# Attention values as four column tiles in one batch per window row, softmax sums inverted once and spread by matmuls

## The chip, the cores and the metric

One NeuronCore of a Trainium2 chip runs the whole program. The time is the device time of one execution in microseconds (us), given as the median of several runs. Engines: TensorE (PE for its matmuls, PEld for its weight loads), VectorE (DVE), ScalarE (ACT), GpSimd (POOL), and SyncE (SP), which only issues DMAs here.

## What is computed

For 32 images of 56x56 pixels with 128 channels, in fp32, two residual blocks one after the other:

```python
x = x + window_attention(group_norm(x))   # 7x7 windows, shifted by 3, 8 heads of 16 channels
x = x + conv3x3(group_norm(x))            # 128 -> 128 channels, weights from signs and clipping
```

Group norm has 32 groups of 4 channels. The attention of one window has N = 49 tokens: `softmax(q k^T / 4 + relative bias + mask) v` for each head, and a 128x128 projection with bias. An image has 8 rows of 8 windows.

## The kernel before, in words

All five engines run one program of images `i` and, in each, 32 units `u`. A unit is one pair of heads (4 pairs) in one row of 8 windows (8 rows). Work of three images is interleaved in a unit: attention of image i, the conv of image i-1, loading and the first norm of image i+1. Every engine has its own `body(i)` with the order of its work written out by hand, and semaphores tie them. TensorE's order in unit u (its `body`, L994 on): scores of two units (only in even u), part of the conv, transposes of the probabilities of unit u-2 (`turn_probs`, L886), the odd jobs placed in the middle of the unit, more conv, then the values of unit u-3 (`values`, L895) before the q, k, v matmuls (`qkv`, L909) in even u and behind them in odd u, more conv, and the odd jobs placed at the end of the unit. Odd jobs (`misc`, L937) share one PSUM bank, `misc_ps`, in a fixed order that `misc_jobs` (L96) lists: turning the attention output ("ot", at u = 7, 11, ...), the projection ("proj", at u = 9, 13, ...), turning loaded and finished tiles ("tin", "tout"), and the group norm's averages ("gn1", "gn2").

The probabilities of a pair of heads lie with 49 queries of an even window at partitions 0 to 48 and of an odd window at 64 to 112. After the transposes `probsT` has, for each window, both heads' 49 keys on the partitions (K of 128 rows, 64 for each head) and 49 queries in the free dimension. `values` takes `probsT` of a window as the weights (128 rows x 49 columns) and V as the moving operand (34 columns: 16 channels of each head, and a column of ones for each head, which gives the softmax sums). Even windows write PSUM partitions 0 to 48, odd ones 64 to 112: two column tiles. After every two pairs VectorE takes reciprocals of the sums (L706) and multiplies (L714, two products), into `o_sb`, tokens on partitions. "ot" transposes `o_sb` of the row by four transposes (L953), ScalarE copies the result to fp16 (`oT_hi`, L472), VectorE makes the remainder (`oT_lo`, L727), and "proj" multiplies with the fp16 weights (high and low parts, three matmuls).

The scores are fp32 with 32 rows x 49 columns of weights and 98 moving columns (L880): two row groups times two column groups of the array. q, k, v and the conv are fp16 in three products (L867, L986). In the trace an fp32 matmul is two pairs of a weight load and a matmul; a transpose and an fp16 matmul are one.

Stores: `x_out` has a slot for each of the 7 tiles of an image; ScalarE copies a finished tile into it (L485) and SP stores it (L352).

Of the kernel before, what the change touches and what calls it, by code (L numbers as in the profile page):

```python
# [26 lines left out]

# [23 lines left out]
VW = 2 * HD + 2  # L51
# [7 lines left out]
SUB = 4  # L59
# [9 lines left out]
LAG_T, LAG_PV = 2, 3  # L69
# [72 lines left out]

def roll_pieces(rows, row0=0):
# [8 lines left out]
def build_block(nc, x, wqkv, bqkv, wproj, bproj, table, wconv, prune, ident_d, group_d, parity_d, mask_d, out):  # L152
    with ExitStack() as ctx:
# [22 lines left out]
        w_in = sb("w_in", [128, 4, C])  # L176
# [3 lines left out]
        w_f = sb("w_f", [128, 4, C])  # L180
# [24 lines left out]
        x_out = sb("x_out", [SP_, TILES * SUB, C])  # L205
# [4 lines left out]
        v = sb("v", [128, 2, NWIN, PAIRS, VW])  # L210
# [46 lines left out]
        x_stored = [sem(f"x_stored{t}") for t in range(TILES)]  # L257
# [13 lines left out]
        attn_norm = sem("attn_norm")  # L271
        oT_hi_ready = sem("oT_hi_ready")
# [21 lines left out]
        wc_u = flat(x_of[1])[:, 0:PLANES * KW * C].rearrange("p (t c) -> p t c", c=C)  # L294
        wc_sum = flat(x_n)[:, 0:C]
# [21 lines left out]
        def _(sp):  # L317
# [24 lines left out]
            def body(i):  # L342
                for u in range(UNITS):
                    for kind, t in misc_at(i, u):
# [4 lines left out]
                        if kind == "tout":  # L349
                            img = i - 1 - tile_turned(t)[0]  # L350
                            sp.wait_ge(misc_free, misc_number(i, kind, t) + 1)
                            sp.dma_start(out_tiles[img, t], x_out[:, t * SUB:(t + 1) * SUB, :]).then_inc(x_stored[t], 16)  # L352

            over_images(sp, body)
            for t in range(TILES):
                sp.wait_ge(x_stored[t], 16 * IMGS)
# [3 lines left out]
        def _(pool):  # L360
# [8 lines left out]
            last.then_inc(rel_ready, 1)  # L369

# [78 lines left out]
        def _(act):  # L449
# [10 lines left out]
            def evacuate_probsT(i, g, slot):  # L460
                act.wait_ge(probsT_ready, g + 1)
                need(act, attn_ready, g - 1)
                nc.scalar.copy(probsT[:, slot % 2], probsT_ps[:].rearrange("p (w n) -> p w n", n=ODD)[:, :, 0:N])\  # L463
                    .then_inc(probsT_sb, 1)

            def misc(i, u, place):
                for kind, t in misc_at(i, u, (place,)):
                    number = misc_number(i, kind, t)
                    if kind == "ot":

                        act.wait_ge(misc_ready, number + 1)
                        nc.scalar.copy(oT_hi[:].rearrange("p r (w c) -> p w r c", c=WIN),  # L472
                                       misc_ps[:].rearrange("p (w n) -> p w n", n=ODD)[:, :, 0:N]
                                       .rearrange("p w (r c) -> p w r c", c=WIN)).then_inc(oT_hi_ready, 1)
# [6 lines left out]
                    if kind == "tout":  # L481
                        img = i - 1 - tile_turned(t)[0]
                        act.wait_ge(misc_ready, number + 1)
                        need(act, x_stored[t], 16 * img)
                        nc.scalar.copy(x_out[:, t * SUB:(t + 1) * SUB, :],  # L485
# [3 lines left out]
            def body(i):  # L489
                for u in range(UNITS):  # L490
# [62 lines left out]
        def _(dve):  # L553
# [12 lines left out]
            for buf, value in ((v, 0.0), (probs, 0.0), (scores_ps, 0.0), (attn_ps, 1.0)):  # L566
# [4 lines left out]
            for e in range(2):  # L571

                step(vec.memset(v[ODD * e:ODD * e + N, :, :, :, 2 * HD + e:2 * HD + e + 1], 1.0))
# [33 lines left out]
            step(vec.tensor_copy(wT_hi[:], w_f[:]))  # L607
            step(vec.tensor_tensor(wT_lo[:], w_f[:], wT_hi[:], ALU.subtract))
# [89 lines left out]
            def body(i):  # L698
                for u in range(UNITS):

                    n, rest = divmod(u - (LAG_PV + 2), 2)
                    if rest == 0 and live(i, 0 if n >= 0 else -1):
                        number, half = i * ROWS * 2 + n, n % 2
                        dve.wait_ge(attn_ready, (number + 1) * 2)
                        outputs = attn_ps[0:QP, 0:WP * 2 * VW].rearrange("p (a v) -> p a v", v=VW)
                        vec.reciprocal(recip[0:QP, half], outputs[:, :, 2 * HD:VW]).then_inc(recip_ready, 1)  # L706
                        dve.wait_ge(recip_ready, number + 1)
                        if half == 0 and (not isinstance(number, int) or number > 0):

                            turn = i if u >= 2 else i - 1  # L710
                            dve.wait_ge(misc_ready, misc_number(turn, "ot", (n // 2 - 1) % ROWS) + 1)
                        for pair in range(2):
                            at = (half * 2 + pair) * 2 * HD
                            last = vec.tensor_tensor(  # L714
                                o_sb[0:QP, :, at:at + 2 * HD].rearrange("p w (e d) -> p w e d", d=HD),
                                outputs.rearrange("p (w a) v -> p w a v", a=2)[:, :, pair, 0:2 * HD]
                                .rearrange("p w (e d) -> p w e d", d=HD),
                                recip[0:QP, half].rearrange("p (w a) e -> p w a e", a=2)[:, :, pair].unsqueeze(3)
                                .to_broadcast((QP, WP, 2, HD)), ALU.mult)
                        last.then_inc(attn_norm, 1)  # L720
                    turn, at = divmod(u - 1, UNITS)
                    for kind, t in misc_at(i + turn, at):
                        if kind == "ot":

                            row = (i + turn) * ROWS + (t if at >= OT_AT else t - ROWS)
                            dve.wait_ge(oT_hi_ready, row + 1)
                            vec.tensor_tensor(oT_lo[:].rearrange("p r (w c) -> p w r c", c=WIN),  # L727
                                              misc_ps[:].rearrange("p (w n) -> p w n", n=ODD)[:, :, 0:N]
                                              .rearrange("p w (r c) -> p w r c", c=WIN),
                                              oT_hi[:].rearrange("p r (w c) -> p w r c", c=WIN), ALU.subtract)\  # L730
                                .then_inc(misc_free, 1)
# [114 lines left out]
        def _(pe):  # L846
# [48 lines left out]
            def values(i, u):  # L895
                g, (r, pair) = i * UNITS + u, divmod(u, PAIRS)
                pe.wait_ge(probsT_sb, g + 1)
                if pair == 0:
                    pe.wait_ge(qkv_free, (i * ROWS + r) * 4 + 4)
                if pair % 2 == 0:  # L900
                    need(pe, attn_norm, (i * ROWS + r) * 2 + pair // 2)
                for w in range(NWIN):
                    p0, wp = ODD * (w % 2), w // 2
                    at = (wp * 2 + pair % 2) * VW
                    last = mm(attn_ps[p0:p0 + N, at:at + VW], probsT[:, u % 2, w, :], v[:, r % 2, w, pair, :],  # L905
                              start=True, stop=True)
# [30 lines left out]
            def misc(i, u, kind, t):  # L937
# [12 lines left out]
                if kind == "ot":  # L950
                    pe.wait_ge(attn_norm, (i * ROWS + (t + 1 if u >= OT_AT else t + 1 - ROWS)) * 2)
# [118 lines left out]
```

## Time and profile before

| | us |
|---|---|
| median of 3 runs | 3638.6 (3636.86 to 3641.4) |
| the profiled execution | 3642.03 |
| its span | 3640.2 |
| matmuls on TensorE | 57227 |
| busy: TensorE, its weight loads | 3423.5 (94%), 2802.9 (77%) |
| busy: VectorE, ScalarE, GpSimd | 3016.5 (83%), 2559.9 (70%), 2293.8 (63%) |

A busy share is the time in which an engine had an instruction under way. Matmul durations are modelled and overlap; their starts are measured. The idle time before a group, with the engine and line that ended it, tells who waited for whom.

### The profile page before, as it was taken

How to read it: one execution, taken by the hardware profiler on the slowest of the kernel's cores; microseconds unless marked ns; L12 is line 12 of the kernel's file. 1: busy time of each engine (PE TensorE's matmuls, PEld its weight loads, DVE VectorE, ACT ScalarE, POOL GpSimd, SP SyncE). 2: the span in 40 equal slices, each digit the busy share in tenths (PEclk: the TensorE clock that was granted, in tenths of full speed). 3: DMA queues.
4: the chain of work that ended last, by engine and by line, in shares of the span. 5: the costliest groups of instructions: out<-in, count | busy, mean ns of one | idle time of the engine just before them, and what ended most of it. 6: DMA issues, size and time to landing. Idle time of an engine off the chain costs nothing.

```text
span 3640.2 us, 140757 instructions
## 1 busy us (share of the span) xinstructions
PE 3423.5 (94%) x57227; PEld 2802.9 (77%) x57227; DVE 3016.5 (83%) x7426; ACT 2559.9 (70%) x5729; POOL 2293.8 (63%) x3674
## 2 busy tenths in 40 slices
PE   2999999999999999999999999999999999999997
PEld 1778778777778777778777778777778778778775
DVE  5788888888888888888888888888888888888875
ACT  1777777777777777777777777777777777777763
POOL 4476666766666766656766666766656766657753
PEclk9999999999999999999999999999999999999999
DMA  2011101111101111101111001111001111101001
GB/s 57 20 30 33 33 25 30 35 33 35 33 25 30 35 33 35 33 23 33 33 35 35 28 28 33 33 35 35 28 28 33 33 35 33 30 25 33 18 18 29
DMA packets 213328, 113.72 MB, mean 31 GB/s; under 512 B 8784, under 2 KB 212688, under 8 KB 212688
## 3 DMA queue, kind: packets, MB, share of 16 engines
q1 hardware_dynamic: 212688, 104.72, 10.1%
q8 instruction: 459, 7.52, 0.8%
q14 instruction: 181, 1.48, 0.1%
HBM read 53.31 MB, written 51.38 MB: 29 GB/s over the span
## 4 chain that ended last, share of the span: by engine, by line
PE 52%; DVE 23%; POOL 12%; issue 10%; ACT 2%; SPq 0%; DVEq 0%; DMA 0%; POOLq 0%; ACTq 0%
PE conv_ps L986 14%; PE qkv_ps L867 11%; PE attn_ps L905 7%; PE probsT_ps L891 7%; PE scores_ps L880 5%; DVE s_sb L738 4%; DVE plane_lo L750 3%; POOL s_sb L402 3%; PE misc_ps L867 2%; DVE x L781 2%; DVE s_max L743 2%; PE misc_ps L953 2%; PE misc_ps L949 2%; PE misc_ps L943 2%; POOL x_n L441 1%
## 5 line engine op out<-in xcount | busy, mean ns | idle before, releaser
L402 POOL TENSOR_TENSOR s_sb<-s_sb,s_max 113x392 f32<-113x392 f32 x1024 | 1000.8, 977 | 1171.4 <-DVE s_max L743 1167.1
L457 ACT ACTIVATE probs<-s_sb 113x392 f32<-113x392 f32 x1024 | 552.4, 539 | 158.4 <-POOL s_sb L402 151.2
L891 PE MATMUL probsT_ps<-ident,probs 113*128 113x113 f32 x4096 | 587.4, 265 | 75.0 <-ACT probsT L463 74.9
L429 POOL TENSOR_TENSOR plane<-x_n 128x224 f32<-128x224 f32 x896 | 600.8, 691 | 18.7
L526 ACT COPY v<-qkv_ps 64x256 f32<-64x256 f32 (+2 forms) x1280 | 393.8, 327 | 300.9 <-PE qkv_ps L867 294.6
L743 DVE TENSOR_REDUCE s_max<-s_sb 113x8 f32<-113x392 f32 x1024 | 574.7, 561 | 35.3
L905 PEld LDWEIGHTS attn_ps<-v,probsT 128*49 128x49 f32 x16384 | 466.0, 125 | 179.0 <-issue 137.4
L463 ACT COPY probsT<-probsT_ps 128x392 f32<-128x392 f32 x1024 | 489.7, 478 | 161.1 <-PE probsT_ps L891 155.8
L738 DVE TENSOR_TENSOR s_sb<-scores_ps,bias 113x392 f32<-113x392 f32 x1024 | 567.6, 554 | 7.6 <-PE scores_ps L880 7.6
L905 PE MATMUL attn_ps<-v,probsT 128*49 128x34 f32 x16384 | 567.2, 214 | 0.4 <-DVE o_sb L714 0.2
L891 PEld LDWEIGHTS probsT_ps<-ident,probs 113*128 113x128 f32 x4096 | 432.6, 142 | 133.7 <-ACT probs L457 87.8
L986 PE MATMUL conv_ps<-plane_hi,wc_hi 128*128 128x224 f16 x2688 | 483.3, 262 | 15.8 <-DVE conv_y L812 11.4
L986 PE MATMUL conv_ps<-plane_hi,wc_lo 128*128 128x224 f16 x2688 | 481.5, 262 | 0.0
L880 PE MATMUL scores_ps<-k,q 32*49 32x98 f32 x16384 | 458.5, 248 | 0.0
L880 PEld LDWEIGHTS scores_ps<-k,q 32*49 32x49 f32 x16384 | 353.3, 119 | 119.8 <-issue 83.4
L986 PE MATMUL conv_ps<-plane_lo,wc_hi 128*128 128x224 f16 x2688 | 409.3, 261 | 18.0 <-DVE plane_lo L750 18.0
L781 DVE SCALAR_TENSOR_TENSOR x<-misc_ps,w_max,x 128x371 f32<-128x371 f32 (+2 forms) x576 | 199.8, 393 | 252.5 <-PE misc_ps L867 252.5
L867 PE MATMUL qkv_ps<-wT_hi,tok_hi 128*128 128x128 f16 (+1 forms) x2304 | 398.2, 227 | 4.4 <-ACT v L526 2.8
L867 PE MATMUL qkv_ps<-wT_lo,tok_hi 128*128 128x128 f16 (+1 forms) x2304 | 389.3, 220 | 0.0
L867 PE MATMUL qkv_ps<-wT_hi,tok_lo 128*128 128x128 f16 (+1 forms) x2304 | 389.3, 220 | 0.0
L441 POOL TENSOR_SCALAR x_n<-x,gn_y,gn_shift 128x371 f32<-128x371 f32 (+2 forms) x576 | 338.4, 597 | 7.6 <-POOL gn_shift L391 7.6
L517 ACT ACTIVATE k<-qkv_ps,k_bias,k_scale 128x392 f32<-128x392 f32 x512 | 321.3, 682 | 13.6 <-PE qkv_ps L867 13.5
(144 smaller groups left out, 6564.2 us busy)
## 6 DMA issues: line engine op xcount, KB each, us to landing
x_in<-in_x_dram SPq DMA_DIRECT2D x224, 224.0 KB, 2.7
out_dram<-x_out SPq DMA_DIRECT2D x224, 224.0 KB, 2.3
x<-in_L_conv_w_dram SPq DMA_DIRECT2D x1, 576.0 KB
x<-L_conv_pruning_mask_dram SPq DMA_DIRECT2D x1, 576.0 KB
x_n<-_conv_rel_pos_table_dram SPq DMA_DIRECT2D x14, 10.7 KB
x_n<-in_mask_dram SPq DMA_DIRECT2D x1, 196.0 KB
w_in<-n_L_conv_qkv_weight_dram SPq DMA_DIRECT2D x1, 192.0 KB
ident<-in_ident_dram SPq DMA_DIRECT2D x1, 64.0 KB
```

What stands on the lines that cost most here:

```text
L402: nc.gpsimd.tensor_tensor(s, s, top, ALU.subtract).then_inc(sub_ready, 1)
L429: last = nc.gpsimd.tensor_tensor(plane[:, t % 2, j], *sums[j])
L457: nc.scalar.activation(probs[0:QP, slot % 2, :, :, 0:N], s_sb[0:QP, slot % 4], ACT.Exp)\
L463: nc.scalar.copy(probsT[:, slot % 2], probsT_ps[:].rearrange("p (w n) -> p w n", n=ODD)[:, :, 0:N])\
L526: last = nc.scalar.copy(v[half, slot, w0:w0 + n, :, e * HD:(e + 1) * HD], vals[half, b:b + n, :, e, :])
L738: vec.tensor_tensor(s_sb[0:QP, u % 4].rearrange("p w h m -> p (w h m)"), scores_ps[0:QP, u % 2, 0:WP * 2 * N], bias[0:QP, edge, u % PAIRS] ...
L743: vec.tensor_reduce(s_max[0:QP, u % 4], s_sb[0:QP, u % 4].rearrange("p w h m -> p (w h) m"), AX.X, ALU.max).then_inc(max_ready, 1)
L867: last = mm(out_ps, w, t, start=(n == 0), stop=(n == 2))
L880: last = mm(scores_ps[p0:p0 + N, (u + n) % 2, (w // 2) * 2 * N:(w // 2 + 1) * 2 * N], q[at, r % 2, w, :], k[at, r % 2, w].rearrange("p e m ...
L891: last = nc.tensor.transpose(probsT_ps[:, w * 128:w * 128 + QP], probs[0:QP, u % 2, w].rearrange("p e m -> p (e m)"), ident[0:QP, 0:QP])
L905: last = mm(attn_ps[p0:p0 + N, at:at + VW], probsT[:, u % 2, w, :], v[:, r % 2, w, pair, :], start=True, stop=True)
L986: last = mm(conv_ps[:, j, 0:PP].rearrange("p (r w) -> p r w", w=W), w[:, j * KW + dx, :], p[:, j, k * TPAIRS:(k + 1) * TPAIRS, dx:dx + W], ...
```

## The change

`values` no longer runs once a unit but once a row of windows, at u = 6, 10, ... (`VALUES_AT`), before the q, k, v matmuls of that unit. V (32 columns of a head pair) is now the weight, `probsT` of a window the moving operand (49 columns); each pair of heads writes its own 32 PSUM partitions, so there are four column tiles, and the output has channels on partitions and tokens in the free dimension. The ones columns are gone from V. The sums come from a second set of matmuls whose weights, `head_ones`, hold for each window one column of ones per head: accumulated over the 8 windows, they put the sums of 4 pairs x 8 windows x 2 heads into rows of one 128 x 49 block beside the values. VectorE inverts that block in one reciprocal. The job "ot" becomes "rec": for each window one fp32 matmul with the weight `head_rows` (128 x 128, a row for each channel's head) spreads the reciprocals over the channels. Meanwhile ScalarE copies the values to SBUF (`values_sb`); VectorE multiplies them with the spread reciprocals from PSUM. `oT_hi` and `oT_lo` are then made from SBUF, the latter one unit later, and "proj" waits for it. `probsT` gets 6 slots in place of 2, `x_out` 2 in place of 7, and the raw projection weights of the setup lie in `plane`'s space. GpSimd makes the two constants in the setup.

```diff
-LAG_T, LAG_PV = 2, 3
+LAG_T = 2
+PT_SLOTS = 6
+VALUES_AT = 6
+OUT_SLOTS = 2
...
-        for first, kind in ((OT_AT, "ot"), (PROJ_AT, "proj")):
+        for first, kind in ((OT_AT, "rec"), (PROJ_AT, "proj")):
...
+def row_of(i, u, first):
+
+    r, rest = divmod(u - first, PAIRS)
+    turn, r = divmod(r, ROWS)
+    return (i + turn) * ROWS + r if rest == 0 and live(i, turn) else None
...
-        v = sb("v", [128, 2, NWIN, PAIRS, VW])
+        v = sb("v", [128, 2, NWIN, PAIRS, 2 * HD])
-        probsT = sb("probsT", [128, 2, NWIN, N])
-        recip = sb("recip", [128, 2, 2 * WP, 2])
-        o_sb = sb("o_sb", [128, WP, C])
+        probsT = sb("probsT", [128, PT_SLOTS, NWIN, N])
+        recip = sb("recip", [128, N])
+        values_sb = sb("values_sb", [128, NWIN, N])
+        o_sb = sb("o_sb", [128, NWIN, N])
...
+            nc.gpsimd.memset(head_ones[:], 0.0).then_inc(head_consts, 1)
...
+                    diagonal = flat(head_ones)[ODD * e:ODD * e + ODD, a * HD + e::2 * HD + 2]
+                    nc.gpsimd.memset(diagonal, 1.0).then_inc(head_consts, 1)
...
+            rows = ident[:].rearrange("k (p x) -> k p x", x=2 * HD)
+            for w in range(NWIN):
+                last = nc.gpsimd.tensor_copy(
+                    head_rows[:, w, :].rearrange("k (p e d) -> k p e d", e=2, d=HD),
+                    rows[:, :, 2 * w:2 * w + 2].unsqueeze(3).to_broadcast((128, PAIRS, 2, HD)))
...
@@ ScalarE
             def evacuate_probsT(i, g, slot):
                 act.wait_ge(probsT_ready, g + 1)
-                need(act, attn_ready, g - 1)
+                if g >= PT_SLOTS:
+                    act.wait_ge(attn_ready, (g - PT_SLOTS) // PAIRS + 1)
...
+                    row = row_of(i, u, VALUES_AT + 2)
+                    if row is not None:
+
+                        act.wait_ge(misc_free, rec_number(row) + 1)
+                        nc.scalar.copy(oT_hi[:].rearrange("p r (w c) -> p w r c", c=WIN),
+                                       o_sb[:].rearrange("p w (r c) -> p w r c", c=WIN)).then_inc(oT_hi_ready, 1)
                     misc(i, u, MID)
+                    row = row_of(i, u, VALUES_AT)
+                    if row is not None:
+
+                        act.wait_ge(attn_ready, row + 1)
+                        if row > 0:
+                            act.wait_ge(misc_free, rec_number(row - 1) + 1)
+                        nc.scalar.copy(values_sb[:], attn_ps[:, 0:RT].rearrange("p (w n) -> p w n", n=N))\
+                            .then_inc(values_copied, 1)
...
@@ VectorE
+                    row = row_of(i, u, VALUES_AT + 1)
+                    if row is not None:
+
+                        dve.wait_ge(attn_ready, row + 1)
+                        dve.wait_ge(values_copied, row + 1)
+                        vec.reciprocal(recip[:], attn_ps[:, RT:RT + N]).then_inc(recip_ready, 1)
+                    row = row_of(i, u, VALUES_AT + 3)
+                    if row is not None:
+
+                        dve.wait_ge(oT_hi_ready, row + 1)
+                        vec.tensor_tensor(oT_lo[:].rearrange("p r (w c) -> p w r c", c=WIN),
+                                          o_sb[:].rearrange("p w (r c) -> p w r c", c=WIN),
+                                          oT_hi[:].rearrange("p r (w c) -> p w r c", c=WIN), ALU.subtract)\
+                            .then_inc(oT_lo_ready, 1)
                     turn, at = divmod(u - 1, UNITS)
                     for kind, t in misc_at(i + turn, at):
-                        if kind == "ot":
+                        if kind == "rec":
...
+                            dve.wait_ge(misc_ready, misc_number(i + turn, kind, t) + 1)
+                            vec.tensor_tensor(o_sb[:], misc_ps[:, 0:RT].rearrange("p (w n) -> p w n", n=N),
+                                              values_sb[:], ALU.mult).then_inc(misc_free, 1)
...
@@ TensorE
+            def values(row):
+
+                if row == 0:
+                    pe.wait_ge(head_consts, 6)
+                pe.wait_ge(probsT_sb, (row + 1) * PAIRS)
+                pe.wait_ge(qkv_free, (row + 1) * 4)
+                need(pe, values_copied, row)
+                need(pe, recip_ready, row)
+                for w, pair in product(range(NWIN), range(PAIRS)):
+                    parts = slice(2 * HD * pair, 2 * HD * (pair + 1))
+                    mm(attn_ps[parts, w * N:(w + 1) * N], v[:, row % 2, w, pair, :],
+                       probsT[:, (row * PAIRS + pair) % PT_SLOTS, w, :], start=True, stop=True)
+                for w, pair in product(range(NWIN), range(PAIRS)):
+                    parts = slice(2 * HD * pair, 2 * HD * (pair + 1))
+                    last = mm(attn_ps[parts, RT:RT + N], head_ones[:, w, :],
+                              probsT[:, (row * PAIRS + pair) % PT_SLOTS, w, :],
+                              start=(w == 0), stop=(w == NWIN - 1))
                 last.then_inc(attn_ready, 1)
...
-                if kind == "ot":
-                    pe.wait_ge(attn_norm, (i * ROWS + (t + 1 if u >= OT_AT else t + 1 - ROWS)) * 2)
-                    for w in range(WP):
-                        last = nc.tensor.transpose(misc_ps[:, w * 128:w * 128 + QP], o_sb[0:QP, w, :], ident[0:QP, 0:QP])
+                if kind == "rec":
+                    pe.wait_ge(recip_ready, i * ROWS + (t + 1 if u >= OT_AT else t + 1 - ROWS))
+                    for w in range(NWIN):
+                        last = mm(misc_ps[:, w * N:(w + 1) * N], head_rows[:, w, :], recip[:], start=True, stop=True)
                 if kind == "proj":
-
+                    pe.wait_ge(oT_lo_ready, i * ROWS + (t + 1 if u >= PROJ_AT else t + 1 - ROWS))
...
-                    late = (u - LAG_PV) % 2 == 0
-                    have_values = live(i, 0 if u >= LAG_PV else -1)
-                    if have_values and not late:
-                        values(i if u >= LAG_PV else i - 1, (u - LAG_PV) % UNITS)
+                    row = row_of(i, u, VALUES_AT)
+                    if row is not None:
+                        values(row)
                     if live(i, 0 if u // PAIRS < ROWS - 1 else 1):
                         qkv(i, u)
-                    if have_values and late:
-                        values(i if u >= LAG_PV else i - 1, (u - LAG_PV) % UNITS)
```

## Rows read from the trace of the kernel before

**Rows 1.** The page's first part: busy time, share of the span and instructions.

```profile
span 3640.2 us, 140757 instructions
...
PE 3423.5 (94%) x57227; PEld 2802.9 (77%) x57227; DVE 3016.5 (83%) x7426; ACT 2559.9 (70%) x5729; POOL 2293.8 (63%) x3674
```

**Rows 2.** Three stretches of one image each: busy time by engine, granted clock, DMA.

```profile
1800.00:1909.60 109.60, 105.48 (x1788) 86.61 (x1786) 91.28 (x227) 78.29 (x177) 69.87 (x112) 1.00 0.11 32
...
2019.20:2128.80 109.60, 105.81 (x1790) 86.96 (x1790) 92.95 (x231) 79.87 (x180) 70.93 (x114) 1.00 0.11 32
```

**Rows 3.** Waits of TensorE: us in total, times, longest.

```profile
PEld probsT_ps L891 <- ACT probs L457: 87.8, 62, 1.8
...
PE probsT_ps L891 <- ACT probsT L463: 74.9, 61, 1.7
```

**Rows 4.** Timeline of weight loads: start us, busy us of the group, instruction.

```profile
1801.46 0.47 PEld L905 LDWEIGHTS attn_ps<-v,probsT 128*49 128x49 f32 x16
1801.97 0.39 PEld L953 LDWEIGHTS misc_ps<-ident,o_sb 113*128 113x128 f32 x4
1802.50 0.69 PEld L880 LDWEIGHTS scores_ps<-k,q 32*49 32x49 f32 x32
1803.32 0.40 PEld L891 LDWEIGHTS probsT_ps<-ident,probs 113*128 113x128 f32 x4
...
1804.06 0.45 PEld L905 LDWEIGHTS attn_ps<-v,probsT 128*49 128x49 f32 x16 [0.19 <-issue]
1804.55 0.10 PEld L867 LDWEIGHTS qkv_ps<-tok_hi,wT_hi 128*128 128x128 f16 x1
```

**Rows 5.** Timeline of matmuls around the batch at 1804.06.

```profile
1803.77 0.36 PE L986 MATMUL conv_ps<-plane_hi,wc_hi 128*128 128x224 f16 x2
1804.06 0.56 PE L905 MATMUL attn_ps<-v,probsT 128*49 128x34 f32 x16
```

**Rows 6.** Chain that ended last, in order of time: start us, us, what.

```profile
1805.62 0.44 PE misc_ps L949 x4
...
1806.35 0.39 PE probsT_ps L891 x4
```

**Rows 7.** Timeline around one average of the group norm, loads and matmuls.

```profile
1509.66 0.30 PEld L964 LDWEIGHTS misc_ps<-gn_var,group 128*128 128x128 f32 x2 [0.92 <-issue]
1509.69 0.35 PE L964 MATMUL misc_ps<-gn_var,group 128*128 128x2 f32 x2 [0.73 <-DVE gn_var L677]
...
1509.90 0.45 PE L986 MATMUL conv_ps<-plane_hi,wc_lo 128*128 128x224 f16 x3
```

**Rows 8.** Timeline of weight loads within V's fp16 matmuls, 128 columns each.

```profile
1800.78 0.10 PEld L867 LDWEIGHTS qkv_ps<-wT_lo,tok_hi 128*128 128x128 f16 x1
1800.84 0.10 PEld L867 LDWEIGHTS qkv_ps<-wT_hi,tok_hi 128*128 128x128 f16 x1
```

**Rows 9.** Groups of instructions: xcount, busy us, mean ns, idle before.

```profile
L738 DVE TENSOR_TENSOR s_sb<-scores_ps,bias 113x392 f32<-113x392 f32 x1024 | 567.6, 554 | 7.6 <-PE scores_ps L880 7.6
L463 ACT COPY probsT<-probsT_ps 128x392 f32<-128x392 f32 x1024 | 489.7, 478 | 161.1 <-PE probsT_ps L891 155.8
L714 DVE TENSOR_TENSOR o_sb<-attn_ps,recip 113x128 f32<-113x128 f32 x1024 | 250.2, 286 | 17.6
L828 DVE TENSOR_TENSOR tok_lo<-x_n,tok_hi 128x392 f16<-128x392 f32 x256 | 185.4, 724 | 10.7 <-ACT tok_hi L536 10.7
L727 DVE TENSOR_TENSOR oT_lo<-misc_ps,oT_hi 128x392 f16<-128x392 f32 x256 | 145.3, 568 | 102.1 <-ACT oT_hi L472 101.7
L706 DVE RECIPROCAL recip<-attn_ps 113x16 f32<-113x16 f32 x512 | 127.3, 249 | 3.0 <-PE attn_ps L905 1.7 <-DVE gn_y L694 0.3
```

**Rows 10.** Setup: GpSimd's small copies, and its wait for VectorE.

```profile
L368 POOL COPY x_n<-x_n 113x8 f32<-113x8 f32 x49 | 6.3, 199 | 3.0 <-DMA x_n<-_conv_rel_pos_table_dram 3.0
...
POOL x L372 <- DVEq L625: 17.9, 1, 17.9
```

**Rows 11.** DMA issues: KB each, median us from issue to landing.

```profile
out_dram<-x_out SPq DMA_DIRECT2D x224, 224.0 KB, 2.3
```

More of the change, by code:

```diff
@@ L26 @@
 from contextlib import ExitStack
+from itertools import product
 import concourse.bass as bass
@@ L140, in misc_at, with rec_number @@
     return [job[1:] for job in misc_jobs(i if isinstance(i, int) else STEADY) if job[0][0] == u and job[0][1] in places]
+def rec_number(row):
+    img, r = divmod(row, ROWS)
+    return misc_number(img + (OT_AT + PAIRS * r) // UNITS, "rec", r)
+def row_of(i, u, first):
+    r, rest = divmod(u - first, PAIRS)
+    turn, r = divmod(r, ROWS)
+    return (i + turn) * ROWS + r if rest == 0 and live(i, turn) else None
 def roll_pieces(rows, row0=0):
@@ L256, in build_block @@
         x_loaded = [sem(f"x_loaded{t}") for t in range(TILES)]
-        x_stored = [sem(f"x_stored{t}") for t in range(TILES)]
+        x_stored = [sem(f"x_stored{slot}") for slot in range(OUT_SLOTS)]
         misc_ready, misc_free = sem("misc_ready"), sem("misc_free")
@@ L294, in build_block @@
         wc_u = flat(x_of[1])[:, 0:PLANES * KW * C].rearrange("p (t c) -> p t c", c=C)
+        early = plane[:].rearrange("p s j r w -> p (s j r w)")
+        w_in, w_f = (early[:, j * 4 * C:(j + 1) * 4 * C].rearrange("p (t c) -> p t c", c=C) for j in range(2))
         wc_sum = flat(x_n)[:, 0:C]
@@ L369, in _ @@
             last.then_inc(rel_ready, 1)
+            nc.gpsimd.memset(head_ones[:], 0.0).then_inc(head_consts, 1)
+            pool.wait_ge(head_consts, 1)
+            for e in range(2):
+                for a in range(2):
+                    diagonal = flat(head_ones)[ODD * e:ODD * e + ODD, a * HD + e::2 * HD + 2]
+                    nc.gpsimd.memset(diagonal, 1.0).then_inc(head_consts, 1)
+                    pool.wait_ge(head_consts, 2 + 2 * e + a)
+            rows = ident[:].rearrange("k (p x) -> k p x", x=2 * HD)
[3 more added lines that the diff above has]
+                    rows[:, :, 2 * w:2 * w + 2].unsqueeze(3).to_broadcast((128, PAIRS, 2, HD)))
+            last.then_inc(head_consts, 1)
             pool.wait_ge(channel_max, 1)
@@ L483, in misc @@
                         act.wait_ge(misc_ready, number + 1)
-                        need(act, x_stored[t], 16 * img)
-                        nc.scalar.copy(x_out[:, t * SUB:(t + 1) * SUB, :],
+                        turn, slot = divmod(img * TILES + t, OUT_SLOTS)
+                        need(act, x_stored[slot], 16 * turn)
+                        nc.scalar.copy(x_out[:, slot * SUB:(slot + 1) * SUB, :],
                                        misc_ps[0:SP_, :].rearrange("p (s c) -> p s c", s=SUB))\
@@ L565, in _ @@
             dve.sem_inc(rel_zeroed, 1)
-            for buf, value in ((v, 0.0), (probs, 0.0), (scores_ps, 0.0), (attn_ps, 1.0)):
+            for buf, value in ((v, 0.0), (probs, 0.0), (scores_ps, 0.0)):
                 vec.memset(buf[:], value)
@@ L570, in _ @@
             step(vec.memset(ones, 1.0))
-            for e in range(2):
-                step(vec.memset(v[ODD * e:ODD * e + N, :, :, :, 2 * HD + e:2 * HD + e + 1], 1.0))
             dve.wait_ge(const_in, 16 * N_CONST)
@@ L699, in body @@
                 for u in range(UNITS):
[L701 to L720, printed above, removed]
@@ L893, in turn_probs @@
                 last.then_inc(probsT_ready, 1)
[L895 to L906, printed above, removed]
+            def values(row):
[14 more added lines that the diff above has]
+                              start=(w == 0), stop=(w == NWIN - 1))
                 last.then_inc(attn_ready, 1)
```

37 lines of the change are left out of this document (14 added, 23 removed).

## Prediction, made before the changed kernel ran

> **What bounds the kernel now.** I read the page's busy table first. TensorE shows 94% of the span, VectorE 83%, ScalarE 70%, GpSimd 63%, at a granted clock of 0.99 to 1.00, which is the 2.4 GHz level [rows 1, 2]. A modelled busy share proves little for TensorE, so the second view is the table of stretches: three images of 109.60 us each hold 105.5 to 105.8 us of TensorE work, 3.8 us of idle each [rows 2]. Third, the list of waits says what that idle is: TensorE waits for the exponentials and for the copied transposed probabilities, 88 us before weight loads and 75 before matmuls, which overlap; that is most of it [rows 3]. TensorE starts its work in program order except across array tiles, and hardly ever waits. So time added to or taken from its stream goes into the span nearly one to one, and the question is what one row of windows (32 images times 8 rows, 256 rows) costs on TensorE before and after.
>
> Fourth, the timeline of weight loads and matmuls [rows 4, 5] gives that. I go by starts, since ends are modelled: the distance from a group's first weight load to the next group's is what it really takes.
>
> **What the change removes, per row.** A values batch (8 windows, 16 instruction pairs of load and matmul, two array tiles side by side) runs from 1804.06 to the next group's 1804.55: 0.49 us [rows 4]. In front of it the two conv matmuls, started at 1803.77 and 0.10 later, would have let the next start at 1803.97: 0.09 us goes for the turn from whole array to tiles [rows 4, 5]. Three of four batches pay 0.58; the one behind V's 64-column matmuls pays no front: 1801.46 to 1801.97, 0.51. Sum 3 x 0.58 + 0.51 = 2.25 us. The four transposes of the output take 1801.97 to 1802.50, 0.53 [rows 4]. Removed: 2.78 us a row.
>
> **What it adds, per row.** Unit prices first. An fp32 matmul is two instruction pairs (16 for 8 windows). Streaming fp32: four transposes of 113 columns take 0.39 us, of 128 columns 0.44 [rows 6], so 0.86 ns a column. The scores, 98 columns, 32 pairs on four tiles (two row groups by two column groups), take at most 0.69 + 0.12 (to 1803.32 with the turn) [rows 4]; 8 steps of 98 x 0.86 = 0.084 are 0.67, so four tiles ran abreast. Weight load: the values batch has 8 loads of 49 columns per tile, the last starting 0.45 - 0.13 = 0.32 us after the first, 0.046 a step, longer than its 34 columns of streaming (0.029): it is bound by loads, 0.9 ns a column. With 128 columns, two fp32 loads of the normalisation are 0.30 us together and 0.19 each, so the second starts 0.11 after the first, though each matmul streams two columns; the conv matmul behind them starts at 1509.90, 0.13 after the second load [rows 7].
>
> The new batch: 8 windows for the values and 8 for the sums, two pairs each, is 32 steps on each of four column tiles. A step is the longer of a 32-column load (0.03) and 49 columns of streaming (0.043): 32 x 0.043 = 1.39. Front 0.09, tail as now (0.49 - 8 x 0.046 = 0.12), 0.01 for the longer last stream: 1.61 us. The trace has no four column tiles over all 128 rows. Bounds: 128 pairs at 0.011 each if all abreast (1.39), at 0.022 each if only two column tiles run at once as in the old batch (2.77). I take the first, as the scores show four chains abreast and the old batch shows column tiles that don't disturb each other.
>
> The Trainium skill (TensorE: Matmul & The Clock Gate, Measured speedup vs the span model) gives 2.38x for three column tiles. By it, the batch would be 1.39 x 3/2.38 = 1.75 us, an estimate, 0.36 more a row and some 93 us in all; no run here shows it.
>
> The spreading ("rec"): 8 fp32 matmuls with a 128-column weight and 49 columns streamed, so 16 loads of 128 columns. By the normalisation's rows, 16 x 0.11 = 1.76. In front V's last stream (0.06, from 1800.78 to 1800.84 [rows 8]) and the turn back to the whole array (0.09); behind it the last stream 0.04 and the turn to the scores 0.09: 2.04 us. Bounds: 16 x 0.043 = 0.69 if loads hid behind streams, and 16 x 0.13 = 2.08. I take 0.11, the same operation in type and shape of weight.
>
> Sum: 1.61 + 2.04 - 2.78 = **+0.87 us a row**, x 256 = **+223 us**. So batching saves three turns and the output transposes, but the sums' 64 extra pairs and above all sixteen fp32 loads of a full weight cost more.
>
> **The other engines.** VectorE loses per row two reciprocals, four products and the low part from PSUM, (127.3 + 250.2 + 145.3)/256 = 2.04 us; it gains one reciprocal of 49 columns (0.25 to 0.3), one product like the bias addition (0.55) and the low part from SBUF (0.57, to 0.72 as the tokens' low part) [rows 9]: 0.5 us less. It isn't the bound, so nothing of it counts. ScalarE gains a copy like that of the transposed probabilities, 0.48 us a row, 122 us in all, to 2683 of some 3850, 70% [rows 1, 9]; its cover is large. Queued behind its wait for the batch are V's copies of the same unit; TensorE needs those one unit later, behind some 20 matmuls and transposes (over 1.5 us): hidden. "rec" waits for the reciprocal at the head of VectorE's next unit, again over 2 us after the batch. VectorE's product waits for "rec" ahead of the next bias addition, but the scores come behind "rec" on TensorE too. Output projection waits for the low part two units after "rec". The two store buffers: ScalarE waits for a store issued eight units (27 us) earlier (8 of the 32 units of an image) that lands in 2.3 us [rows 11]: nothing. SP's queue has the same stores. Setup: 13 GpSimd operations, at 0.2 [rows 10] to 0.8 us each, 3 to 10 us; GpSimd waits 17.9 us there for VectorE's channel maximum [rows 10], so nothing, or 10 us if that cover is gone.
>
> **Idle given back.** Of 3.8 us of idle an image, what waits for chains on ScalarE, VectorE and GpSimd shrinks as TensorE gets 7 us longer an image; but units now differ in length (two 0.6 shorter, two about 1.0 longer), which makes new waits in the short ones. I take 0.5 us back an image: -15 us, between 0 and -100.
>
> Profiled execution 3642.0 us + 223 - 15 = 3850. The median of the runs shown is 3.4 lower: **3847 us**. Runs of one kernel agree to about 0.1%, so 0.2%, 7 us, is what can be told from no change.
>
> **Rivals.**
> - *Loads that hide.* If the spreading's loads went at the pace of its streams (0.043), a row costs 0.87 - 16 x 0.067 = -0.20 us, -52 us in all: 3575 with the idle. It decides from below 0.055 a load, where the row breaks even. For it: in the transposes a 128-column fp32 load hides behind 113 columns of streaming (0.097 a step) [rows 4, 6]. Against it: the normalisation's pairs stream next to nothing and still stand 0.11 apart, 128 in all [rows 7]. Chance 0.06 of faster; 0.03 that it lands near no change.
> - *Tiles two at a time.* The batch takes 2.77 + 0.22: +1.38 a row, 353 us: 4200. For it: each partition must feed four streams where it fed two. Against: scores. Chance 0.10.
> - *TensorE can't be fed.* 128 pairs at 0.011 is twice the densest stretch of now (scores, 32 pairs in 0.65 to 0.69, 0.02 each). At 0.02 the batch is 2.6 us, +1.2 a row, 310 us: 4160; if the queue in front covers part, about 3950. For it: no stretch shows more. Against: within a burst the first pairs start a few ns apart, and both dense stretches are explained by loads or streams. Chance 0.20.
> - *TensorE's floor.* Tiles might not overlap in issue at all. At the fastest pace one array shows for small work, 0.043 a pair, 128 pairs take 5.5 us, +4.1 a row: 4900. Scores at 0.02 a pair speak against it. Chance 0.02. The Trainium skill (TensorE: Matmul & The Clock Gate, Wait — 56ns, not 53.3ns?) states that matmul starts are never under about 25 ns apart. By that the batch would be 3.2 us and the time about 4310, an estimate; the scores' 20 ns say that the rule doesn't bind across tiles.
> - *Idle refilled.* All of the idle absorbed, and other engines no longer late: 3642 + 223 - 100 = 3765. Chance 0.10.
>
> The forecast as worked out, within 60 us, has 0.49. Faster by over 0.2%: 0.06; within: 0.03; slower: 0.91. The range leaves out the hiding loads, the tiles two at a time and the full feed limit: 3740 to 4090.
>
> **What would show it.** Matmuls of values and sums: 32768, batch from first load to the next group 1.5 us. "rec" 4096 matmuls, starts 0.11 apart. TensorE's image 7 us longer, idle under 3.8. VectorE busy down by 130 to 170 us, ScalarE up by 120. The prediction is wrong if the batch stands well above 1.6 us, if "rec" takes nearer 0.7 than 1.8, or if TensorE's idle grows by more than 1 us an image.

## The result and the profile after

The changed kernel takes 3867.3 us (median of 4 runs, 3864.2 to 3871.6) against 3639.2 us: a ratio of 1.063, 95% interval 1.061 to 1.065. The profiled execution took 3865.3 us, 223 more than the profiled one of before. The forecast was 3847.

The first part of the page after; TensorE has 19456 matmuls more, VectorE is as busy as before in microseconds:

```profile
span 3863.5 us, 179390 instructions
...
PE 3657.3 (95%) x76683; PEld 3153.2 (82%) x76683; DVE 3039.8 (79%) x6399; ACT 2658.9 (69%) x5985; POOL 2344.6 (61%) x3687
```

Three stretches of one image each, now 116.5 us, with TensorE, its loads, VectorE, ScalarE and GpSimd in this order. TensorE's work in an image is 112.4 to 113.8 us where it was 105.5 to 105.8 [rows 2]:

```profile
1800.00:1916.50 116.50, 113.79 (x2411) 98.47 (x2413) 94.03 (x199) 83.47 (x189) 72.77 (x115) 1.00 0.11 31
1916.50:2033.00 116.50, 112.37 (x2389) 97.50 (x2380) 92.85 (x198) 81.74 (x186) 71.15 (x112) 1.00 0.10 29
2033.00:2149.50 116.50, 112.52 (x2389) 97.40 (x2387) 92.50 (x197) 81.81 (x185) 71.54 (x112) 1.00 0.11 31
```

The timeline of weight loads for one row of windows, which answers to [rows 4] (L940 values, L944 sums, L902 V's matmuls, L993 the spreading, L915 scores):

```profile
2005.02 0.79 PEld L940 LDWEIGHTS attn_ps<-probsT,v 128*32 128x32 f32 x64 [0.18 <-issue]
2005.72 0.80 PEld L944 LDWEIGHTS attn_ps<-probsT,head_ones 128*32 128x32 f32 x64
2006.59 0.10 PEld L902 LDWEIGHTS qkv_ps<-wT_hi,tok_hi 128*128 128x128 f16 x1
...
2010.06 1.86 PEld L993 LDWEIGHTS misc_ps<-recip,head_rows 128*128 128x128 f32 x16
2011.98 0.69 PEld L915 LDWEIGHTS scores_ps<-k,q 32*49 32x49 f32 x32
```

The batch takes 2005.02 to 2006.59, 1.57 us, and the spreading 2010.06 to 2011.98, 1.92 us, over two thirds of the 2.78 us that all the removed work took. From the starts of all 256 rows: the batch has a median of 1.566 us but a mean of 1.793, because 52 of the 256 hold a pause, 48 of them before a load of the sums. The list of waits names those 48, and shows that TensorE's other waits shrank (88 and 75 us in [rows 3]):

```profile
PEld attn_ps L944 <- issue: 45.3, 48, 1.8
...
PEld probsT_ps L926 <- ACT probs L494: 34.0, 41, 1.9
...
PE probsT_ps L926 <- ACT probsT L501: 26.3, 49, 1.7
```

One such pause: loads stop after 60 of 64 and come back 1.67 us after the last one's modelled end, released by nothing that the profile shows:

```profile
276.14 0.78 PEld L944 LDWEIGHTS attn_ps<-probsT,head_ones 128*32 128x32 f32 x60
278.59 0.14 PEld L944 LDWEIGHTS attn_ps<-probsT,head_ones 128*32 128x32 f32 x4 [1.67 <-issue]
```

The page's list of DMA queues has one that carries instructions, 7.52 MB in 459 packets before, now

```profile
q8 instruction: 612, 10.03, 1.1%
```

that is 16 KB a packet; with some 153000 loads and matmuls in 10 MB, a packet is about 256 instructions, just what a batch issues (128 loads and 128 matmuls) in 1.4 us. Each of the 52 pauses ended 2.2 to 3.1 us after the start of such a packet, while the ends of all batches lie anywhere from 0.1 to 6.1 us behind one (5th and 95th percentile). Packets started at least 3.3 us apart.

### The profile page after: what moved, and what is told of

It is laid out like the page before. It is cut to its first block, busy times and chain, and to the rows that moved or that the text cites. A ratio compares the mean times of both kernels' runs of the same rounds, so it can differ in the third digit from the quotient of the medians.

```text
span 3863.5 us, 179390 instructions
## 1 busy us (share of the span) xinstructions
PE 3657.3 (95%) x76683; PEld 3153.2 (82%) x76683; DVE 3039.8 (79%) x6399; ACT 2658.9 (69%) x5985; POOL 2344.6 (61%) x3687
## 4 chain that ended last, share of the span: by engine, by line
PE 77%; POOL 9%; DVE 7%; issue 5%; ACT 2%; SPq 0%; DMA 0%; POOLq 0%; ACTq 0%; DVEq 0%
PE conv_ps L1026 17%; PE qkv_ps L902 14%; PE misc_ps L993 11%; PE scores_ps L915 9%; PE probsT_ps L926 9%; PE attn_ps L940 5%; PE attn_ps L944 5%; PE misc_ps L902 3%; POOL s_sb L439 2%; PE misc_ps L983 2%; DVE s_sb L773 2%; PE misc_ps L989 2%; DVE s_max L778 1%; POOL gn_t L425 1%; POOL x_n L478 1%
## 5 line engine op out<-in xcount | busy, mean ns | idle before, releaser
L466 POOL TENSOR_TENSOR plane<-x_n 128x224 f32<-128x224 f32 x896 | 628.4, 722 | 18.7
L773 DVE TENSOR_TENSOR s_sb<-scores_ps,bias 113x392 f32<-113x392 f32 x1024 | 556.0, 543 | 74.4 <-PE scores_ps L915 74.2
L993 PE MATMUL misc_ps<-recip,head_rows 128*128 128x49 f32 x4096 | 509.1, 277 | 0.2 <-DVE gn_ve L734 0.2
L993 PEld LDWEIGHTS misc_ps<-recip,head_rows 128*128 128x128 f32 x4096 | 477.3, 192 | 23.6 <-DVE gn_ve L734 0.4
L915 PE MATMUL scores_ps<-k,q 32*49 32x98 f32 x16384 | 458.1, 248 | 0.0
L915 PEld LDWEIGHTS scores_ps<-k,q 32*49 32x49 f32 x16384 | 353.0, 119 | 97.5 <-issue 72.3
L902 PE MATMUL qkv_ps<-wT_hi,tok_hi 128*128 128x128 f16 (+1 forms) x2304 | 397.2, 226 | 17.5 <-ACT v L573 8.3
L902 PE MATMUL qkv_ps<-wT_hi,tok_lo 128*128 128x128 f16 (+1 forms) x2304 | 388.1, 220 | 4.9 <-issue 4.9
L902 PE MATMUL qkv_ps<-wT_lo,tok_hi 128*128 128x128 f16 (+1 forms) x2304 | 388.2, 220 | 3.8 <-issue 3.6
L552 ACT COPY values_sb<-attn_ps 128x392 f32<-128x392 f32 x256 | 125.5, 490 | 285.7 <-PE attn_ps L944 285.7
```

The costliest lines, as they stand in the source:

```text
L466: last = nc.gpsimd.tensor_tensor(plane[:, t % 2, j], *sums[j])
L773: vec.tensor_tensor(s_sb[0:QP, u % 4].rearrange("p w h m -> p (w h m)"), scores_ps[0:QP, u % 2, 0:WP * 2 * N], bias[0:QP, edge, u % PAIRS] ...
L902: last = mm(out_ps, w, t, start=(n == 0), stop=(n == 2))
L915: last = mm(scores_ps[p0:p0 + N, (u + n) % 2, (w // 2) * 2 * N:(w // 2 + 1) * 2 * N], q[at, r % 2, w, :], k[at, r % 2, w].rearrange("p e m ...
L993: last = mm(misc_ps[:, w * N:(w + 1) * N], head_rows[:, w, :], recip[:], start=True, stop=True)
```

## Experiments

**Without the sums.** What are the sums' matmuls worth?

```diff
-            for buf, value in ((v, 0.0), (probs, 0.0), (scores_ps, 0.0)):
+            for buf, value in ((v, 0.0), (probs, 0.0), (scores_ps, 0.0), (attn_ps, 1.0)):
...
-                for w, pair in product(range(NWIN), range(PAIRS)):
-                    parts = slice(2 * HD * pair, 2 * HD * (pair + 1))
-                    last = mm(attn_ps[parts, RT:RT + N], head_ones[:, w, :],
```

> The changed kernel without the 32 matmuls of the softmax sums (their PSUM columns hold 1.0 from the setup, so the values are not normalised). TensorE theory: 16 of 32 steps of 0.043 us go, 0.69 us a row, 177 us; the long pauses inside the batch (0.23 us a row on average, put down to issue) go too if they come from instructions that arrive too slowly, 58 us: 3865 - 235 = 3630 us, a little more if waits for other engines come back. If the pauses come from somewhere else they stay, 3690. If TensorE isn't the bound, less than 100 us goes.

3735.6 us, a single run, 130 less and not 235. The batch falls to a mean of 0.853 us with no pause, as expected. But this kernel's clock isn't whole: 0.95 in the first stretch, 1.00 in the second.

```profile
3300.00:3400.00 100.00, 97.22 (x1641) 83.66 (x1640) 79.38 (x166) 71.66 (x162) 61.00 (x100) 0.95 0.11 32
1796.60:2011.60 215.00, 208.84 (x3699) 179.52 (x3697) 181.17 (x388) 160.36 (x363) 137.86 (x218) 1.00 0.11 32
```

The images that ran wholly at 2.4 GHz took 109.9 to 110.3 us; those with 6.8 us at 1.2 GHz 113.1, those with 10.2 us 114.7 to 115.1. The changed kernel's images take 116.5 on average. So at full clock the sums and their pauses are worth 6.5 us an image, 208 in all, of the 7.5 by which the stream is shorter. Only 130 show in the time: this kernel ran 212 us at 1.2 GHz, the changed one 33, and at 3.1 us for 6.8 that is some 82 us, an estimate.

**The same count of instructions, no sums.** Do the pauses belong to the sums or to the burst?

```diff
-                for w, pair in product(range(NWIN), range(PAIRS)):
+                for again, w, pair in product(range(2), range(NWIN), range(PAIRS)):
```

on top of the kernel without the sums.

> The changed kernel with the sums' 32 matmuls replaced by a second pass of the 32 values matmuls (the PSUM columns of the sums hold 1.0, the values are not normalised): the same number of instructions and the same step, no accumulation and no constant weights. Feed theory (a burst of 256 instructions outruns their fetch): the pauses inside the batch stay, mean distance from the batch's first load to the next group's near 1.79 us with a median near 1.57, time within 15 us of 3867. Rival, the pauses belong to the sums' accumulation or their weights: mean falls to the median, 3867 - 58 = 3810 us or less.

3879.6 us, a single run; the batch has a median of 1.565 and a mean of 1.826 us. The pauses are there without any accumulation and without `head_ones`:

```profile
PE attn_ps L940 <- issue: 50.2, 53, 1.9
```

**Batch in two halves.**

```diff
                         qkv(i, u)
+                    if row is not None:
+                        sums(row)
                     conv(i, u, 2)
```

`sums` holds the second loop of `values` and its increment.

> The changed kernel with the sums' matmuls behind the V matmuls of the same unit, so the two halves of the batch stand apart by 0.8 us of fp16 work. Feed theory (256 instructions in 1.4 us are more than is fetched in that time): pauses inside the two halves fall from 58 us in all to under 15; against it stands one more turn between whole array and tiles, 0.09 + 0.14 us a row, 59 us. Together 3865 us, within 20. Rival, the pauses belong to the accumulating matmuls of the sums (most stand within them): they stay, 3925 us.

3893.7 us, ratio 1.070 (1.068 to 1.071) to the kernel before, 26 us over the changed kernel; the forecast's upper edge was 3885. The values half has no pause (mean 0.853); in the sums half 0.10 us a row is left (mean 0.956, median 0.854), 26 us where it was 58. The extra turn costs its 57 us, so the balance is plus 26: the arithmetic holds, but nearly half of the pauses stayed. Together with the run before: it is the burst, not the kind of work, and 0.8 us between its two halves (64 loads and 64 matmuls each) are not enough to cure it.

**The loops turned round.**

```diff
-                for w, pair in product(range(NWIN), range(PAIRS)):
+                for pair, w in product(range(PAIRS), range(NWIN)):
```

in both loops.

> The changed kernel with the loops of the batch turned round: all 8 windows of one pair of heads, then the next pair, so that 16 instruction pairs in a row go to the same column tile. Theory that the four tiles run abreast only because consecutive matmuls go to different ones, within the little that TensorE looks ahead: up to 0.043 us for each of 128 pairs, the batch 5.5 us in place of 1.4, the time up to 4900 us, and somewhere between if it looks ahead by more than 16 pairs. Rival, each tile takes its own matmuls from however far ahead: 3865 us, no change.

4578.2 us, a single run. The same 128 pairs, in another order, take 2011.79 to 2016.53:

```profile
2011.79 2.34 PEld L940 LDWEIGHTS attn_ps<-probsT,v 128*32 128x32 f32 x62 [0.18 <-issue]
...
2014.14 2.32 PEld L944 LDWEIGHTS attn_ps<-probsT,head_ones 128*32 128x32 f32 x61
2016.53 0.10 PEld L902 LDWEIGHTS qkv_ps<-wT_hi,tok_hi 128*128 128x128 f16 x1
```

4.74 us in place of 1.57: 0.037 a pair, near the 0.043 that 49 columns of streaming take on one tile. With neighbours in program order on different tiles all four run abreast; with 16 pairs in a row for each tile they hardly overlap. The mean batch (4.742) stands on its median (4.736): at this pace the same instructions bring no pause. That is the third run on the side of slow fetching. It rests on three runs and on the times of the packets; no record says what TensorE's queue was short of. The time rose by 713 us (of the profiled executions) where the batches grew by 755, so here nearly all arrived.

**The kernel before with a longer stream.** Where did part of the added stream go?

```diff
-                    for w in range(WP):
+                    for n in range(3 * WP):
+                        w = n % WP
```

in "ot".

> The kernel before, with the output's four transposes of a row done three times over (same result). Adds 8 x 0.0965 = 0.77 us of TensorE stream a row, 198 us, and nothing for the other engines. If a longer stream by itself takes up idle time (theory for the 2 us an image that the changed kernel idles less): 3640 + 130 to 160 = 3770 to 3800 us. Rival, the idle fell because VectorE and the order of the work changed: the whole 198, 3838 us.

3748.8 us, ratio 1.030 (1.028 to 1.031): 107 us more, where 198 us of stream were added (the group went from 0.54 to 1.31 us). Even less came through than I thought. An image takes 113.1 us, TensorE's idle in it is 1.8 us or less, of 3.8 before:

```profile
1800.00:1913.10 113.10, 111.28 (x1852) 92.89 (x1850) 92.88 (x230) 79.26 (x179) 70.74 (x113) 1.00 0.11 31
2000.00:2113.10 113.10, 111.60 (x1854) 93.25 (x1853) 93.17 (x230) 79.60 (x180) 71.10 (x114) 1.00 0.11 31
```

TensorE's idle was waiting for chains on the other engines; a longer stream walks into that time by itself, with nothing else changed, and no change in VectorE's load is needed for it. Of the 91 us that didn't arrive, some 70 are this idle (2.0 to 2.3 us an image). The rest isn't separated; the padded kernel also ran 23 us at 1.2 GHz where the kernel before ran 50.

**Spreading in fp16.**

```diff
+                        dve.wait_ge(recip_raw, row * 2 + 1)
+                        vec.tensor_copy(recip_hi[:], recip[:]).then_inc(recip_raw, 1)
+                        dve.wait_ge(recip_raw, row * 2 + 2)
+                        vec.tensor_tensor(recip_lo[:], recip[:], recip_hi[:], ALU.subtract).then_inc(recip_ready, 1)
...
-                        last = mm(misc_ps[:, w * N:(w + 1) * N], head_rows[:, w, :], recip[:], start=True, stop=True)
+                        mm(misc_ps[:, w * N:(w + 1) * N], head_rows[:, w, :], recip_hi[:], start=True, stop=False)
+                        last = mm(misc_ps[:, w * N:(w + 1) * N], head_rows[:, w, :], recip_lo[:], start=False, stop=True)
```

`head_rows` is fp16 here.

> The changed kernel with the spreading in fp16: VectorE splits the 49 columns of reciprocals in a high and a low part (two small instructions more), and each window has two fp16 matmuls with the same 128-column fp16 weight, so still 16 pairs a row. Theory that the spreading is bound by its sixteen fp32 loads of 0.11 us: a pair falls to the 0.056 of V's fp16 matmuls, the group from 1.92 to about 1.05 us, 0.87 us a row and 223 us of stream; the padded kernel gave back 46% of such a change as idle, so 100 to 223 us less: 3645 to 3765. Rival, the price is the pair's own (issue or 49 columns): no change, 3867, or some us more for VectorE.

3728.3 us, ratio 1.025 (1.024 to 1.027): 139 us less than the changed kernel, still 90 more than before. Still 16 pairs, but now 0.025 us apart:

```profile
2009.28 0.10 PEld L999 LDWEIGHTS misc_ps<-recip_hi,head_rows 128*128 128x128 f16 x1 [0.28 <-issue]
...
2009.66 0.10 PEld L1000 LDWEIGHTS misc_ps<-recip_lo,head_rows 128*128 128x128 f16 x1
2009.79 0.69 PEld L921 LDWEIGHTS scores_ps<-k,q 32*49 32x49 f32 x32
```

The group fell from 1.92 to 0.51 us, 361 us of stream, more than the 223 expected: an fp16 pair of 49 columns is half of V's 0.056. So the price of the spreading is its fp32 type, load and stream together; the next run parts the two. But only 139 of the 361 us arrived: TensorE's waits for the exponentials and copies are back (96 and 84 us), and the batch stands 0.35 us a row over its median (mean 1.916, median 1.569). Part of that is the clock: 20 of the 256 batches touch a stretch at 1.2 GHz and take 2.58 us on average. The other 236 have a mean of 1.860, so the pauses themselves grew from 0.22 to 0.29 us a row.

```profile
PEld probsT_ps L932 <- ACT probs L496: 96.3, 55, 2.9
...
PE probsT_ps L932 <- ACT probsT L503: 83.9, 61, 2.8
...
PEld attn_ps L950 <- issue: 55.0, 65, 2.0
```

Between 1000 and 3300 us TensorE idles 164 us in this kernel, 67 in the changed kernel and 80 in the kernel before. At 1.2 GHz it spends 104 us in all, the changed kernel 33. The images without such a stretch take 111.9 us against 116.5, which is 147 us in all: at full clock too only 41% arrives, so what is missing is idle in the main.

**One wide fp32 matmul.**

```diff
+                        vec.tensor_tensor(recip_wide[:], recip[:].unsqueeze(1).to_broadcast((128, NWIN, N)),
+                                          head_mask[:].unsqueeze(2).to_broadcast((128, NWIN, N)), ALU.mult)\
+                            .then_inc(recip_ready, 1)
...
-                        last = mm(misc_ps[:, w * N:(w + 1) * N], head_rows[:, w, :], recip[:], start=True, stop=True)
+                    last = mm(misc_ps[:, 0:RT], head_sum[:], recip_wide[:].rearrange("k w n -> k (w n)"),
+                              start=True, stop=True)
```

> The changed kernel with the spreading in one fp32 matmul of 392 columns: VectorE first lays the reciprocals out over the 8 windows with a mask (one product of 128x392, SBUF to SBUF, about 0.56 us a row), and one constant 128x128 weight spreads them. Stream theory: two loads of 0.11 and two streams of 0.34 in place of sixteen loads, the group from 1.92 to about 0.87 us, 1.05 us a row, 268 us of stream; as 46% can return as idle: 3600 to 3720 us. Rival, VectorE (79% busy, here 143 us more) is late with the wide reciprocals or the scores' bias, and little is gained: over 3800.

3757.0 us, ratio 1.033 (1.031 to 1.034): 110 us less, outside both ranges. The group is as worked out:

```profile
2010.13 0.30 PEld L1005 LDWEIGHTS misc_ps<-recip_wide,head_sum 128*128 128x128 f32 x2 [0.43 <-DVE gn_ve L742]
2010.99 0.69 PEld L927 LDWEIGHTS scores_ps<-k,q 32*49 32x49 f32 x32 [0.56 <-ACT v L570]
```

0.86 us, 270 us of stream saved. This run parts load from stream: the same 784 fp32 columns pass (2 x 392 for 16 x 49), behind 2 loads in place of 16, and the group falls by 1.06 us. So the price of the spreading is its fp32 weight loads. 41% of the saving arrived, as with fp16 (39%). VectorE's wide product took 0.62 us a row.

**The same with GpSimd laying out.** The only change is `nc.gpsimd` for `vec` in that product, behind a wait for the reciprocal.

> As the one before, with the laying out on GpSimd (61% busy; about 0.9 us a row, 230 us more), behind the subtraction of the unit before. If VectorE's load is what limits the version before, this one is faster than it by up to 50 us; if GpSimd's subtractions are then late for the exponentials (the wait that TensorE's idle hangs on), it is slower than it by 20 to 100 us. I expect the second: 3650 to 3780 us.

3832.0 us, ratio 1.052 (1.050 to 1.055): 75 us slower than with VectorE, the side that I expected and beyond its range. The reason that I gave doesn't show. The exponentials wait less for GpSimd's subtractions (120 us against 176) and TensorE less for the exponentials (72 against 90); new is TensorE's wait of 71 us for GpSimd's wide reciprocals. Its granted clock was 0.964: it ran 275 us at 1.2 GHz where the version with VectorE ran 81. At 3.1 us for 6.8, as without the sums, the 194 more are worth some 88 us, an estimate, so the clock alone can account for the 75. Why it fell more often isn't shown.

**Fp16 spreading and the split.** Diffs as in the two above.

> The fp16 spreading together with the sums behind V's matmuls. In the fp16 kernel the pauses inside the batch are 0.35 us a row (mean 1.92, median 1.57), 89 us in all. Feed theory: the split leaves some 0.1 us a row as in the split kernel, so 64 us less stream, against 57 us for the extra turn: 3728, within 15. If the pauses hide in TensorE's idle anyway, only the turn shows: 3728 + 30 to 57.

3772.2 us, ratio 1.036 (1.034 to 1.038): 44 us more, in the rival's range. What the batch stands over its median fell only from 0.35 to 0.20 us a row, 37 us, against 57 for the extra turn: 20 us of stream more. The other 24 us stay open.

**Fp16 spreading, the low part later.**

```diff
                             .then_inc(biased, 1)
+                        low_part(i, u)
```

`low_part` is the product into `oT_lo` with its wait, taken from the head of the unit.

> The fp16 spreading with VectorE's low part of the output placed between the bias addition and the maximum of its unit, where GpSimd has less left of the last subtraction. Theory that this product takes 0.94 us in place of 0.57 because GpSimd reads SBUF at the same time: it falls to under 0.8 us. Theory that VectorE's load limits the fp16 kernel (85% busy): 10 to 50 us less than 3728. Rival, VectorE's load isn't what TensorE waits for, and the maximum comes later instead: no change or up to 20 us more.

3725.6 us, ratio 1.024 (1.022 to 1.025): no change against 3728.3, though the product fell from 936 to 765 ns, 44 us of VectorE's time.

```profile
L748 DVE TENSOR_TENSOR oT_lo<-o_sb,oT_hi 128x392 f16<-128x392 f32 x256 | 195.9, 765 | 1.7 <-ACT oT_hi L545 1.7
```

VectorE's load as such isn't what holds the fp16 kernel up. What does, beyond the waits named, stays open; none of the kernels tried is as fast as the one before.

## Why the prediction was right, step by step

**The bound.** That stream time on TensorE goes into the span "nearly one to one" was the weakest sentence. It came out right here only as a sum. Of what was added, 107 of 198 us arrived in the kernel before (54%) and 713 of 755 in the changed kernel (94%). Of what was taken from the changed kernel, some 40% arrived for the spreading and, at full clock, 208 of 240 us (87%) for the sums. So the share isn't one number, and what sets it isn't shown. The idle of 3.8 us an image that the sum starts from is the lower of two values: the first stretch of [rows 2] leaves 4.1.

**Batch.** 1.52 us predicted without the front, 1.566 measured as the median. The four column tiles run abreast over all 128 rows, which no row of before had shown. The two-at-a-time rival is out: the trace has 1.57, it needed 2.9. The estimate after the Trainium skill (TensorE: Matmul & The Clock Gate, Measured speedup vs the span model: 2.38x for three tiles) had 1.75 us for its steps, and the trace doesn't agree: they took 1.39 to 1.43.

**Spreading.** 2.04 predicted with both turns; measured 0.09 + 0.06 in front and 1.92: 2.06. The fp32 load of 0.11 us, read from two loads of the group norm, decided it, and the kernel with one wide fp32 matmul shows that it is the load.

**Per row.** 0.09 + 1.566 + 0.147 + 1.916 - 2.79 = +0.93 us without pauses, +0.87 predicted: 238 us against 223. The 2.79 is for what was removed, between 2.77 from the medians of its groups over the whole trace and 2.80 from their means.

**What I had not in the sum.** The pauses, 0.227 us a row, 58 us. The rival "TensorE can't be fed" had the cause half right and the form wrong: the pace within a burst holds 0.011 a pair, no floor of 0.02; in 52 of 256 the burst stops for up to 1.8 us, and that it runs dry of instructions is argued from the runs above. The prediction called itself wrong if the batch stood well above 1.6 us: the median doesn't, the mean of 1.79 does by the pauses.

**Idle given back.** I took 15 us of a range of 0 to 100; the balance gives 238 + 58 - 223 = 73 us. In an image 3.6 us are idle, of which pauses are 1.8; the other 1.8 stand against 3.8 before. These two misses, +58 and -58, cancel. That is luck: nothing in the prediction ties them together, and without the second the time would have stood 78 us above the forecast, outside the 60 us that the worked-out forecast allowed itself. So the costs per row were right for the stated reasons, and the total was closer (20 us) than its parts.

**VectorE.** Predicted 130 to 170 us less, measured 23 more. The step that failed is the price of two new operations:

```profile
L755 DVE TENSOR_TENSOR oT_lo<-o_sb,oT_hi 128x392 f16<-128x392 f32 x256 | 257.1, 1004 | 27.1 <-ACT oT_hi L543 27.1
...
L765 DVE TENSOR_TENSOR o_sb<-misc_ps,values_sb 128x392 f32<-128x392 f32 x256 | 144.8, 566 | 163.0 <-PE misc_ps L993 158.0
...
L750 DVE RECIPROCAL recip<-attn_ps 128x49 f32<-128x49 f32 x256 | 119.5, 467 | 158.2 <-ACT values_sb L552 154.7 <-DVE gn_y L738 0.3
```

The reciprocal of 49 columns is 0.47 us, not 0.25 to 0.3: against 0.25 for 16 columns [rows 9], 6.6 ns a column. The low part is 1.00 us, not 0.57 to 0.72. With them the three new groups take 521.4 us and the three that went took 522.8, so nothing is saved. The 23 us on top stand in no price: VectorE's instructions overlap less than before. None of it seems to have mattered for the time: 44 us less of VectorE's work in the last experiment changed nothing. **ScalarE** rose by 99 us, 120 predicted. Stores, setup and the queues showed nothing, as said; TensorE's waits for ScalarE's copies of q and v, which I called hidden, rose from 25 to 43 us.

## What to carry to other kernels

Price each new TensorE group by the longer of its weight load and its stream, in the type that it has: a 128-column fp32 weight for 49 columns of work is paid for by the load, and in fp16 the same spreading cost a quarter. Let small matmuls for different column tiles alternate in program order: with 16 in a row for each tile the same batch took three times as long. A burst of some 256 instructions in 1.4 us can stop on its way, by these runs because their supply falls behind, so batching small matmuls has a price that a sum of durations doesn't show. Time added to the bounding engine is partly taken up by its idle and time taken away is partly returned as idle; the share ran from 40 to 94% here, so padding the old kernel once tells it for that one change and not for the next. Compare the time spent at 1.2 GHz before putting a difference down to the edit.

## What was new about the hardware

- Bursts and supply: 52 of 256 batches paused, up to 1.8 us, each until 2.2 to 3.1 us after an instruction packet's start, and none when the same instructions took 4.74 us.
- Order and tiles: 1.57 against 4.74 us for the same 128 pairs.
- Two operands in SBUF beside GpSimd: in 254 of 256 rows the low part overlapped a GpSimd instruction and took 1.01 us on average, in the other two 0.57. Its time goes with what GpSimd's running instruction had left: 0.57 us where that was under 0.2, 0.98 for 0.4 to 0.6, and 1.21 for 0.7 to 0.8, so it did little until that one had ended. Placed later in the fp16 kernel, where GpSimd had at most 0.6 left, it fell from 0.94 to 0.77 on average. The Trainium skill (SBUF — State Buffer, SBUF: two separate sides) says that such a VectorE operation and a GpSimd one that reads SBUF lock each other out; the trace agrees, and the prediction would have done well to apply it.
- Smallest fp16 pair on the whole array: 0.025 us. The Trainium skill (TensorE: Matmul & The Clock Gate, Wait — 56ns, not 53.3ns?) has about 25 ns between starts as a floor; here the trace agrees, while across four column tiles pairs start 0.011 apart.
- Clock: the kernels differ in their time at 1.2 GHz, 33 us in the changed one, 104 with fp16 spreading, 212 without the sums, 275 with GpSimd laying out. Without the sums 6.8 us of it cost an image 3.1 us. What brings it on isn't shown.
